# Loading the next group's transposed hidden states: during the last down-projection pass, or at the head of the group that uses them

## The reference

```
x = x + layernorm(mixer(layernorm(x)))                 # stage A of the kernel
h = layernorm(x)                                       # stored by stage A as hb_d, bf16
w = softmax(h @ router_w), top 4 of 8 kept, renormalised
y = sum over 8 experts e of  w[e] * (silu(h @ gate_w[e]) * (h @ up_w[e])) @ down_w[e]
  + (silu(h @ s_gate_w) * (h @ s_up_w)) @ s_down_w     # shared expert, 2048 wide
x = x + layernorm(y)                                   # stage B of the kernel
```

## Time and profile before

| | |
|---|---|
| time, median of 2 runs | 7782.43 us (7731.94 to 7832.93) |
| profiled execution, time | 7752.56 us |
| its span on the slowest core (core 2) | 7751.0 us |
| spans of the 8 cores | 7717.5 to 7751.0 us |
| mean granted TensorE clock, by core | 0.731 to 0.735 |
| TensorE matmul busy | 3618.6 us, 47% of the span |
| VectorE busy | 2210.3 us, 29% |
| ScalarE busy | 1332.5 us, 17% |
| GpSimd busy | 582.3 us, 8% |

### The profile page before, as it was taken

One profiled execution on the slowest core, in us unless ns is written; L12 is line 12 of the kernel. 1 busy time (PEld: TensorE's weight loads), 2 busy tenths in 40 slices (PEclk: granted clock), 3 DMA queues, 4 the chain that ended last, 5 costly groups with the idle time before them and its releaser, 6 DMA issues.

```text
span 7751.0 us, 53804 instructions; the slowest of 8 cores (7717.5 to 7751.0 us)
## 1 busy us (share of the span) xinstructions
PE 3618.6 (47%) x14748; PEld 1426.9 (18%) x15046; DVE 2210.3 (29%) x3625; ACT 1332.5 (17%) x2322; POOL 582.3 (8%) x590
## 2 busy tenths in 40 slices
PE   0033333333333333333333333348778787787977
PEld 0010110110111111111111110123333333333333
DVE  0033243243243243243243243221222212221121
ACT  0011121121021121121121121121212112121121
POOL 1001001001001001001001001000000000000000
PEclk9985565565565565565565565579889898898888
DMA  9921211211211211211211211243332433324331
GB/s 108 114 60 31 49 58 31 49 58 31 49 55 34 49 55 34 49 55 34 49 55 34 49 58 31 49 147 109 136 114 98 147 109 136 114 98 147 105 129 66
DMA packets 401960, 578.63 MB, mean 75 GB/s; under 512 B 227024, under 2 KB 309616, under 8 KB 375424
## 3 DMA queue, kind: packets, MB, share of 16 engines
q1 hardware_dynamic: 325776, 392.59, 16.6%
q0 software_dynamic: 75888, 182.58, 11.4%
HBM read 501.75 MB, written 139.98 MB: 83 GB/s over the span
## 4 chain that ended last, share of the span: by engine, by line
PE 39%; DVE 21%; issue 10%; ACT 9%; DMA 8%; SPq 6%; another core or an unknown queue 4%; DVEq 1%; ACTq 1%; POOL 0%; POOLq 0%
PE PA L1137 9%; PE PB L1147 9%; SPq L830 3%; DVE Mp L717 3%; PE PA L1232 2%; PE PB L1232 2%; PE PD L1232 2%; PE PC L1232 2%; DVE tmp1k L245 2%; ACT es L711 2%; PE PA L546 2%; DMA x_d<-x_t 2%; DVE xdt L245 2%; PE PC L729 1%
## 5 line engine op out<-in xcount | busy, mean ns | idle before, releaser
L476 PE MATMUL PA<-lnuT,W_in_sb 128*128 128x512 bf16 x1131 | 396.1, 514 | 986.4 <-DMA lnuT<-lnu_d 677.0
L1137 PE MATMUL PA<-hT,gw 128*128 128x512 bf16 x3002 | 778.3, 403 | 5.9 <-issue 3.2
L1147 PE MATMUL PB<-hT,uw 128*128 128x512 bf16 x3014 | 747.8, 389 | 4.0 <-issue 0.4
L311 DVE TENSOR_REDUCE stat<-PA 128x1 f32<-128x1024 f32 x16 | 19.6, 1225 | 1324.1 <-PE PD L1232 671.8
L729 PE MATMUL PC<-xdt,Mp 128*128 128x64 bf16 x1024 | 94.9, 232 | 636.8 <-DVE Mp L717 636.8
L1147 PEld LDWEIGHTS PB<-hT,uw 128*128 128x128 bf16 x3072 | 309.1, 101 | 391.0 <-issue 69.7
L1137 PEld LDWEIGHTS PA<-hT,gw 128*128 128x128 bf16 x3072 | 306.9, 102 | 399.9 <-issue 99.7
L717 DVE SCALAR_TENSOR_TENSOR Mp<-es,CBTm 128x512 bf16<-128x512 bf16 x256 | 199.0, 777 | 632.4 <-ACT es L711 632.4
L476 PEld LDWEIGHTS PA<-lnuT,W_in_sb 128*128 128x128 bf16 x1152 | 130.4, 121 | 1248.6 <-issue 1202.2
L1160 ACT ACTIVATE sgs<-PA 128x512 bf16<-128x512 f32 x384 | 229.3, 597 | 693.6 <-PE PA L1137 631.6
L702 PE MATMUL PB<-rhsE,lhsE 66*128 66x512 bf16 x256 | 156.7, 612 | 398.1 <-DVE CBTm L690 398.1
(11 more groups left out here) (252 smaller groups left out, 4836.2 us busy)
## 6 DMA issues: line engine op xcount, KB each, us to landing
gw<-gate_bd SPq DMA_DIRECT2D x64, 1024.0 KB
uw<-up_bd SPq DMA_DIRECT2D x64, 1024.0 KB
de<-down_bd SPq DMA_DIRECT2D x36, 1024.0 KB
u_t<-u SPq DMA_DIRECT2D x64, 512.0 KB
wout_b<-W_outT POOLq DMA_DIRECT2D x128, 256.0 KB, 10.0
gw<-sg_bd SPq DMA_DIRECT2D x32, 1024.0 KB
uw<-su_bd SPq DMA_DIRECT2D x32, 1024.0 KB
de<-sd_bd SPq DMA_DIRECT2D x32, 1024.0 KB
```

The source lines that it names most:

```text
L476: fn = lambda e, f=fc, k=kc, b=bank, gb=gb: e.matmul(b.ap, W_inT[:, k * DPROJ + DIN + f * 128: k * DPROJ + DIN + (f + 1) * 128], lnuT[gb][ ...
L1137: fn = lambda e, i=ic, k=kc, b=bkg, w=wb, ss=hs: e.matmul(b.ap, gw[w][:, k * 512 + i * 128:k * 512 + (i + 1) * 128], hT[ss][k], start=(k = ...
L1147: fn = lambda e, i=ic, k=kc, b=bku, w=wb, ss=hs: e.matmul(b.ap, uw[w][:, k * 512 + i * 128:k * 512 + (i + 1) * 128], hT[ss][k], start=(k = ...
```

## The change

One flag is turned over:

```diff
@@ -31,7 +31,7 @@
 NPE = 12
 EPS_LN = 1e-5
 EPS_RMS = 1e-12
-PRE_HT = True
+PRE_HT = False
 PRE_GU = True
 PRE_DE4 = True
 TWT_PD7 = False
```

## The result

| | before | after |
|---|---|---|
| time, median of all runs | 7839.63 us (42 runs, 7721.4 to 8135.98) | 7877.63 us (44 runs, 7772.01 to 8231.82) |
| profiled execution, spans of the 8 cores | 7717.5 to 7751.0 us | 7727.1 to 7794.5 us |
| TensorE's 7 waits between groups, mean of the 8 cores | 258.8 us (252.7 to 267.2) | 309.9 us (299.6 to 322.5) |
| from the first router matmul to the end, mean of the cores | 2592.0 us | 2638.8 us |

The ratio of after to before is 1.009, with a 95% interval of 1.0057 to 1.0123: on the profiled execution's 7752.6 us that is 70 us more (44 to 95). Many runs of both kernels have cores of one die at a lower clock and take longer; they are in the medians of the table and not in the ratio.

What follows compares the result with a forecast made beforehand. TensorE bounds stage B, with 7 gaps of 37.0 us hanging on the `de4` loads. Removal 0 plus 7 x 4.4 = 30.8 us, added to 7752.6, gave 7783.4 us; 8-in-10 range 7740 to 7870 us.

Steps and rivals of the forecast that it cites:

- The 4.4 us a gap: Gap between groups: DMA engine work of the 8 moved transposes, added to the already busy `de4` stretch; 7 x 4.4 = 30.8 us.
- the sign of being wrong: Gaps between groups: the prediction is wrong if the gap grows by more than 7 us.
- the three bounds: How much later than `de4` the transposes land: issue alone 0, engines' work 4.4 us, wholly behind 12.0 us a gap.
- the third bound: Gap between groups: if nothing of the transposes moves until `de4` has landed, 12.0 us are added.
- the stretched issues of stage A: Stage A: 8 transposes beside 8 loads on POOL's queue need 21.7 us from first issue to reader.
- the stage-A bound: Gap between groups: with stage A's 21.7 us from first issue to reader, transposes land 9.1 us after `de4`.
- The removal: Start of pass 2: without 8 transposes, SP's later issues go about 10.3 us earlier, worth nothing; costed at 0.
- The wait was put down to `hT`: Sign ahead of the router matmuls: TensorE's wait is put down to `hT`, not `de4`; 7 waits sum to 290 us.
- Hidden after all: Rival, gap between groups: transposes fit into the engines' gaps and land with `de4`; no change, 7752.6 us; chance 0.12.
- the case above 2%: Rival, gap: transposes start only when `de4` is in and need 22.6 us; 158 us, 7911 us; chance 0.05.
- behind `de4`, or slowed by it: Rival, gap between groups: 9.1 to 12.0 us for each gap, 64 to 84 us, 7816 to 7837 us; chance 0.15.
- The clock rival: Rival, TensorE's matmul stretches: a low-clock spell stays away and gives back 21.3 us, 7762 us; chance 0.08.

Runs made afterwards that it cites:

- the fence: Changed kernel, with SP made to wait until the `de4` loads have landed before it issues the 8 transposes; sum of TensorE's 7 waits 342.8 us, mean of the cores.

## Why the prediction was wrong

The range ended at 7870 us and the median came out at 7877.63. Two steps failed, one in the sum and one in its base.

**The 4.4 us a gap.** This is the term that was mis-sized: it is 7.3 us in the mean of the cores (51.1 / 7), 7.6 on core 2, between 5.4 and 9.1 by core. It is also more than the 7 us which the prediction itself named as the sign of being wrong. The step that failed is the choice among the three bounds: the engines' work is added and nothing else, since "all eight are issued by 5448.1 + 10.3 = 5458.4, before `de4` is in". They weren't. Four were issued by 5461.8, and 0.07 of 1.05 MB had moved when `de4` was in. What was added is not work squeezed into full engines but the rest of the transposes behind `de4`, 8.0 us in this gap of core 2 instead of the 12.0 of the third bound, because part of the issue was done. The row that told this stood in the prediction, the stretched issues of stage A. I set it aside since those transposes ran beside another queue's loads that cast. With `de4` on another queue (309.3) the cost stayed what it was, so another queue was no reason to set it aside; what the cast adds wasn't tested. Against the mean of the cores the stage-A bound, 9.1 us, is 1.8 us too high and my choice 2.9 too low.

The 4.4 was read too low besides. The pass-2 window of the earlier trace rows ends before the transposes do: it holds 3799 of the 4352 packets of a set, 0.92 of 1.05 MB, so its 4.1 us is 4.6 for the set. Alone a set takes 4.6 us there, 4.6 in stage A (38.7% of 12.0 by queue) and 4.8 behind the fence. The 4.0 us for 1 MB, the estimate by the 261 GB/s of the Trainium skill ("DMA: Bandwidth & Descriptors", Latency and other measured facts), is thus less than this kernel's transposes take alone, and the prediction's "agrees" rested on the window cut short. On their own queue beside `de4` they took 6.0.

**The base.** I added the loss to the time of one execution, 7752.6 us, and took the two runs at hand for the spread of medians. With 42 runs the median of before is 7839.6 us, 87 above that base and 57 above the median of the two. 7839.6 with my 30.8 gives 7870.4, already at the range's end, while 7752.6 with the 51.1 us of the waits gives 7803.7, well inside. The median lies 94.2 us above my 7783.4, and 87.1 of that are the base. The two medians differ by 38.0 us, near my 31; that is luck, since the ratio says 70 (44 to 95), the waits 51, and the profiled executions 43.

**What held.** The gap is where the time went, 51.1 us of it against 46.8 in all of stage B. The removal was worth 0: `de4` was issued 0.4 us from where it was, and pass 2 kept its 7.07 us a bank. The wait was put down to `hT`. The bounds 0 and 12.0 held as bounds; the fence confirmed the latter with 342.8 us against the 343 expected for it. "Hidden after all" fell, and so did the case above 2%. The rival "behind `de4`, or slowed by it" was right in kind, though its lower end of 323 us was too high: even core 4, the highest, has 322.5. The clock rival wasn't tested by a run of its own. In the mean the profiled execution shows little of it: the cores' part from the first router matmul grew by 46.8 us where the waits grew by 51.1. On single cores it is there. Core 2's waits grew by 53.2 us and its stage B by 36.7, and the period that had stood at 0.85 before stands at 0.88 after, 341.1 us instead of 344.2 with the longer gap in it:

```profile
7112.60:7453.70 341.10, 271.64 (x1172) 118.12 (x1196) 67.79 (x150) 66.78 (x116) 2.13 (x4) 0.88 0.34 114
```

The 0.82 in the earlier trace rows came while TensorE was busy, so it is no case of what the prediction cited on the time after a pause.

**What stays open.** Why SP's issues are stretched while the engines are full, by whatever queue, and why with two loads they stay stretched after `de4` is in. Why transposes in company take 6.0 us of the engines instead of 4.8. The runs show the conditions, not the mechanism.

## What to carry to other kernels

A transfer that is moved into a stretch with full DMA engines costs what is left of it when the large transfer has landed, and that can be nearly all of it. Look for a row in which the same kind of transfer ran beside other traffic, in any stage and on any queue, and take that one. A window from which an engine's work is read must hold the whole transfer; the packets and bytes of its queue tell. In a gap that hangs on a chain of loads, order the queue by what is needed for the next start and issue the big load first, at the moment its buffer is free: that took 34 us off the waits here, where moving the small ones cost 51. And the base of a forecast is the median, not one execution; with a few runs of before, the spread of that median belongs into the range.

## What the runs showed of the hardware

- Eight transposes of 128 KB issue in 10.3 us alone, in 10.65 behind one load of 1 MB, in 16.0 behind two and in 18.9 behind four (core 2, first gap). The step comes between one load and two. Plain loads of 1 MB show stretched issues too, 4.21 and 4.77 us.
- Behind one, two or four such loads, 0.07 to 0.08 of the transposes' 1.05 MB move until the loads are in; on a queue of their own beside four loads, 0.33.
- Their packets take 4.6 to 4.8 us of the 16 engines alone, and 6.0 on their own queue beside four loads.
- It makes no difference for the 7 waits whether those loads are issued on the same queue or on ScalarE's: 309.9 and 309.3 us.
- Eight plain loads of the same 128 KB cost 4.9 us a gap behind `de4`, more than a fourth of the 15 us that `de4`'s 4 MB take.
